# Causal self-attention: eleven score fills of the row maxima issued between the tiles of the projection

## The reference, cut to what matters

```python
def _attn(x, ln_w, ln_b, conv_w, attn_w, proj_w, n_head):
    h = _layernorm(x, ln_w, ln_b)
    ...
    qkv = h @ attn_w
    q, k, v = jnp.split(qkv, 3, axis=-1)
    ...
    q = q * cos + _rotate_half(q) * sin
    k = k * cos + _rotate_half(k) * sin
    scores = jnp.einsum('bqhd,bkhd->bhqk', q, k) / jnp.sqrt(jnp.float32(D))
    scores = jnp.where(causal, scores, jnp.float32(-1e+30))
    p = jax.nn.softmax(scores, axis=-1)
    y = jnp.einsum('bhqk,bkhd->bqhd', p, v).reshape(B, T, C)
    return y @ proj_w
```

## Time and profile before

| | |
|---|---|
| median of 3 runs | 2651.42 us (2646.68 to 2652.11) |
| the profiled execution | 2654.03 us |
| its span | 2652.2 us |
| mean granted clock of PE | 0.958 |
| PE, DVE, ACT, POOL busy | 85%, 74%, 69%, 50% of the span |
| projection, second half, batch 0 | 1682 to 1696.5 us |
| maxima, batch 0 | 1696.5 to 1786.6 us |
| projection, batch 1 | 1889 to 1926 us |
| maxima, batch 1 | 1926 to 2015.3 us |

### The profile page before, as it was taken

How to read it: one execution, slowest core, us unless ns; L and a number is a source line. 1 busy time by engine, 2 the same in 40 slices (tenths; PEclk the granted TensorE clock), 3 DMA queues, 4 the chain that set the end, 5 groups by cost and what they waited for, 6 DMA issues and landing times. The chain is left out here.

```text
span 2652.2 us, 38396 instructions
## 1 busy us (share of the span) xinstructions
PE 2257.2 (85%) x12302; PEld 1165.0 (44%) x12303; DVE 1974.4 (74%) x1868; ACT 1819.6 (69%) x2842; POOL 1328.6 (50%) x508
## 2 busy tenths in 40 slices
PE   7788888888888888888888897779978979999988
PEld 2344444444434444444444352323422255665547
DVE  6899999999978999999999458782384142225665
ACT  5899999999959999999999335207604731113256
POOL 2099998999942999989999212000000022110020
PEclk8899999999999999999999979879988979999999
DMA  2510001000015000010000012001000051001000
GB/s 91 139 44 28 28 28 40 28 28 27 24 74 135 29 26 25 28 41 27 28 28 21 18 48 84 1 1 38 28 1 25 25 231 69 24 22 38 0 10 32
DMA packets 57112, 110.27 MB, mean 42 GB/s; under 512 B 13123, under 2 KB 18499, under 8 KB 55984
## 3 DMA queue, kind: packets, MB, share of 16 engines
q1 hardware_dynamic: 48656, 97.58, 11.7%
q0 software_dynamic: 8352, 11.31, 1.5%
HBM read 84.97 MB, written 23.59 MB: 41 GB/s over the span
## 5 line engine op out<-in xcount | busy, mean ns | idle before, releaser
L1522 POOL TENSOR_TENSOR hs<-hs,c_bc 128x2048 f32<-128x2048 f32 x256 | 1166.7, 4557 | 60.5 <-DVE hs L1573 45.0
L1573 DVE TENSOR_TENSOR_SCAN hs<-decays,ps 128x512 f32<-128x512 f32 x512 | 610.9, 1216 | 28.8 <-ACT decays L1536 10.0
L1573 DVE TENSOR_TENSOR_SCAN hs<-decays,carry,ps 128x512 f32<-128x512 f32 x512 | 621.5, 1269 | 5.7 <-PE ps L1600 4.7
L1608 PE MATMUL ps<-hs,sel 128*64 128x512 f32 x2048 | 496.3, 605 | 16.7 <-POOL hs L1522 16.4
L1600 PE MATMUL ps<-ident,dbu_even 128*128 128x128 f32 x2048 | 296.3, 283 | 97.5 <-DVE hs L1573 64.1
L1600 PE MATMUL ps<-ident,dbu_odd 128*128 128x128 f32 x2048 | 294.8, 283 | 92.4 <-DVE hs L1573 61.5
L1536 ACT ACTIVATE decays<-delta_far,A 128x512 f32<-128x512 f32 x512 | 359.3, 715 | 7.3 <-DVE hs L1573 7.2
L1536 ACT ACTIVATE decays<-delta_near,A 128x512 f32<-128x512 f32 x512 | 360.2, 716 | 1.8 <-DVE hs L1573 1.8
L1544 ACT ACTIVATE dbu_odd<-du_turned,b_turned 128x512 f32<-128x512 f32 x512 | 359.5, 715 | 0.0
L1544 ACT ACTIVATE dbu_even<-du_turned,b_turned 128x512 f32<-128x512 f32 x496 | 348.4, 715 | 0.0
L1600 PEld LDWEIGHTS ps<-ident,dbu_even 128*128 128x128 f32 x2048 | 220.1, 142 | 248.1 <-DVE hs L1573 192.9
(11 more groups left out here) (338 smaller groups left out, 2623.4 us busy)
## 6 DMA issues: line engine op xcount, KB each, us to landing
c_bc<-c_rows SPq DMA_DIRECT2D x256, 128.0 KB, 2.9
o_rows<-osb SPq DMA_DIRECT2D x26, 256.0 KB
u_rows<-u SPq DMA_DIRECT2D x4, 1024.0 KB, 4.5
d_rows<-delta SPq DMA_DIRECT2D x4, 1024.0 KB, 4.2
delta_near<-d_rows SPq DMA_DIRECT2D x4, 1024.0 KB, 10.1
hs<-u_rows SPq DMA_DIRECT2D x4, 1024.0 KB, 6.7
delta_far<-d_rows SPq DMA_DIRECT2D x4, 1024.0 KB, 12.9
w_down<-in_expert_proj SPq DMA_DIRECT2D x1, 4096.0 KB, 31.8
```

The source lines that it names most:

```text
L1522: pool.tensor_tensor(x, x, spread(c_bc[:, g, :], 4), ALU.mult).then_inc(weighed.sem, 1)
L1573: dve.tensor_tensor_scan(hs[:, quad % RING, n, :], decays[:, s % RING, :], ps[:, DBU + s % RING, :], carry[:, at(i * GB, g), blk] if q els ...
L1608: mm = pe.matmul(ps[lo:lo + DB, ACC + quad % 2 * 2 + j // 2, :], k.sel2[:, :], hs[:, quad % RING, j, :], start=False, stop=False, skip_gro ...
```

## The change

The first eleven fills (those of query tiles 0 to 3) leave `maxima` and are issued inside `project`: fill f goes on PE right behind tile 13 + f, and its reduction on DVE right behind the take of that same tile. All eleven use banks 4 to 7, so the ring of the tiles is cut to banks 0 to 3. The first fill waits for the eight masked copies of the first half on ACT; each later fill waits for the reduction of the fill before it. `maxima` then starts with the fills of tile 4, and its transposition of the first maxima comes after two fills. The place of the normalisation of batch 0 (ahead of tile 8) stays. `negmax` is allocated earlier.

```diff
-def project(k, tiles, banks=8, pending=None, beside=()):
+def project(k, tiles, banks=8, pending=None, beside=(), ahead=None):
...
+    turn_of_pending = min(own, banks)
+    if ahead:
+        banks = ahead.bank
...
                 mm.then_inc(summed.sem, 1)
+                if ahead:
+                    ahead.by_tensor(pe, n)
...
-                elif pending and n == min(own, banks):
+                elif pending and n == turn_of_pending:
...
                         copy(eng).then_inc(followed.sem, 1)
+                if ahead and name == "dve":
+                    ahead.by_vector(eng, n)
...
+class EarlyFills:
+
+    def __init__(self, k, job, negmax, first, copies):
+        self.k, self.jobs, self.negmax, self.first, self.copies = k, [job], negmax, first, copies
+        self.fills = [fill for fill in plan_fills([job], T, True) if (fill[1] + 1) * P <= W]
+        self.scores_to = scores_by(self.fills)
+        self.bank = 8 - STRIPS
+        self.scored, self.maxed, self.followed = k.sig("scored"), k.sig("maxed"), k.sig("followed")
+
+    def by_tensor(self, pe, n):
+        f = n - self.first
+        if not 0 <= f < len(self.fills):
+            return
+        if f:
+            pe.wait_ge(self.maxed.sem, self.maxed.at(f))
+        else:
+            pe.wait_ge(self.followed.sem, self.followed.at(self.copies))
+        score_fill(self.k, pe, self.jobs, self.fills[f], self.bank, self.scored)
+
+    def by_vector(self, dve, n):
+        f = n - self.first
+        if not 0 <= f < len(self.fills):
+            return
+        dve.wait_ge(self.scored.sem, self.scored.at(self.scores_to[f]))
+        reduce_fill(self.k, dve, self.fills[f], self.bank, self.negmax).then_inc(self.maxed.sem, 1)
...
-def maxima(k, jobs, nk, causal, prob, negmax, later, ctx):
+def maxima(k, jobs, nk, causal, prob, negmax, first_fill, later, ctx):
...
+    fills = plan_fills(jobs, nk, causal)[first_fill:]
     PART = NJ * TILES // 2
-    early = 2 + max(f for f, (e, t, *_) in enumerate(fills) if e * TILES + t < PART)
+    early = 2 + max([f for f, (e, t, *_) in enumerate(fills) if e * TILES + t < PART], default=0)
...
-        project(k, tiles, pending=pending, beside=taps(HN, hcs, vec, 0) if b == 0 else ())
+        ahead = EarlyFills(k, job, negmax, len(tiles) // 2 + 1, 4 * C)
+        project(k, tiles, pending=pending, beside=taps(HN, hcs, vec, 0) if b == 0 else (), ahead=ahead)
```

More of the change, by code:

```diff
@@ L754, in _ @@
                 pending.fetch(sp)
+    if ahead:
+        ahead.passed()
     summed.passed(len(tiles))
@@ L1647, in __init__, with attention @@
         self.q, self.kk, self.v, self.out, self.masked = q, kk, v, out, False
-def attention(k, jobs, nk, causal, recip, root, lag, wo, ctx, beside=(), by_pe=0):
+def attention(k, jobs, nk, causal, recip, root, lag, wo, ctx, beside=(), by_pe=0, ahead=None):
     nc, ps = k.nc, k.ps
@@ L1666, in attention @@
     pick = k.sb("pick", [P, 2, 2, P], ctx=ctx) if by_pe else None
-    negmax = k.sb("negmax", [P, len(jobs), T // P, H], ctx=ctx)
+    negmax = ahead.negmax if ahead else k.sb("negmax", [P, len(jobs), T // P, H], ctx=ctx)
     later = MaxRows(k, jobs, negmax, rows, [k.sig(f"max_in{n}") for n in range(2)])
-    maxima(k, jobs, nk, causal, prob, negmax, later, ctx)
+    maxima(k, jobs, nk, causal, prob, negmax, len(ahead.fills) if ahead else 0, later, ctx)
     rows_turned, rows_copied = k.sig("rows_turned"), k.sig("rows_copied")
@@ L1943, in put_rows, with plan_fills @@
               .then_inc(self.max_in[part].sem, 16)
-def maxima(k, jobs, nk, causal, prob, negmax, later, ctx):
+STRIPS = 4
+def plan_fills(jobs, nk, causal):
+    fills = []
+    for e in range(len(jobs)):
+        for t in range(T // P):
+            n = (t + 1) * P if causal else nk
+            for o in range(0, n, W):
+                m = min(W, n - o)
+                per = 4 if m <= W // 4 else 2 if m <= W // 2 else 1
+                for g in range(0, 4, per):
+                    fills.append((e, t, o, m, W // per, range(g, g + per), causal and o + m == n))
+    return fills
@@ new lines, in scores_by, with score_fill @@
+def scores_by(fills):
+    return [STRIPS * sum(len(fill[5]) for fill in fills[:f + 1] if fill) for f in range(len(fills))]
+def score_fill(k, pe, jobs, fill, bank, scored):
+    ps = k.ps
+    e, t, o, m, room, groups, masked = fill
+    qx, kx = jobs[e].qx, jobs[e].kx
+    whole = masked and m == P
+    for j in range(STRIPS if whole else 0):
+        pe.matmul(ps[:, bank + j, :].rearrange("p (g n) -> p g n", g=W // P), k.ident16[:],
+                  spread(k.late_key[:], W // P), start=True, stop=False, skip_group_check=True)
+    for n, group in enumerate(groups):
+        c, par = divmod(group, 2)
+        at = n * room
+        for j in range(STRIPS):
+            strip = slice(32 * j, 32 * j + 32)
+            mm = pe.matmul(ps[:, bank + j, at:at + m], qx[strip, par, c, t * P:(t + 1) * P],
+                           kx[strip, par, c, o:o + m], start=not whole, stop=True, skip_group_check=whole)
+            if whole or not masked:
+                mm.then_inc(scored.sem, 1)
+        for j in range(STRIPS if masked and not whole else 0):
+            pe.matmul(ps[:, bank + j, at + m - P:at + m], k.ident16[:], k.late_key[:],
+                      start=False, stop=True, skip_group_check=True).then_inc(scored.sem, 1)
@@ new lines, in reduce_fill, with passed @@
+def reduce_fill(k, dve, fill, bank, negmax):
+    e, t, o, m, room, groups, _ = fill
+    per = len(groups)
+    banks = k.ps[:, bank:bank + STRIPS, 0:per * room].rearrange("p j (g n) -> p j g n", g=per)
+    to = negmax[:, e, t, :].rearrange("p (g j) -> p j g", j=STRIPS)
+    return dve.tensor_reduce(to[:, :, groups[0]:groups[0] + per], banks[:, :, :, 0:m], AX.X, ALU.max, negate=True)
+class EarlyFills:
[20 more added lines that the diff above has]
+        reduce_fill(self.k, dve, self.fills[f], self.bank, self.negmax).then_inc(self.maxed.sem, 1)
+    def passed(self):
+        self.scored.passed(self.scores_to[-1])
+        self.maxed.passed(len(self.fills))
@@ L1959, in maxima @@
     to_mask = [job for job in jobs if not job.masked]
[L1960 to L1968, removed]
+    fills = plan_fills(jobs, nk, causal)[first_fill:]
     PART = NJ * TILES // 2
-    early = 2 + max(f for f, (e, t, *_) in enumerate(fills) if e * TILES + t < PART)
+    early = 2 + max([f for f, (e, t, *_) in enumerate(fills) if e * TILES + t < PART], default=0)
     fills.insert(early, None)
     NF = len(fills)
-    scores_to = [STRIPS * sum(len(fill[5]) for fill in fills[:f + 1] if fill) for f in range(NF)]
+    scores_to = scores_by(fills)
     with ExitStack() as c2:
@@ L2008, in _ @@
                     continue
-                e, t, o, m, room, groups, masked = fill
-                qx, kx = jobs[e].qx, jobs[e].kx
+                e, t, o, _, _, groups, _ = fill
                 if to_mask and (t, o, groups[0]) == (0, 0, 0):
@@ L2015, in _ @@
                     pe.wait_ge(maxed.sem, maxed.at(f - 1))
[L2016 to L2031, removed]
+                score_fill(k, pe, jobs, fill, STRIPS * (f % 2), scored)
         @block.vector
@@ L2042, in _ @@
                     continue
[L2043 to L2047, removed]
                 dve.wait_ge(scored.sem, scored.at(scores_to[f]))
-                dve.tensor_reduce(to[:, :, groups[0]:groups[0] + per], banks[:, :, :, 0:m], AX.X, ALU.max,
-                                  negate=True).then_inc(maxed.sem, 1)
+                reduce_fill(k, dve, fill, STRIPS * (f % 2), far if fill[2] else negmax).then_inc(maxed.sem, 1)
             if WIDE:
```

4 lines of the change are left out of this document (2 added, 2 removed).

## The result

| | before | changed |
|---|---|---|
| median of 6 runs | 2652.14 us (2646.68 to 2654.34) | 2669.22 us (2664.09 to 2671.88) |
| profiled execution, its span | 2654.03, 2652.2 us | 2671.88, 2670.1 us |
| mean granted clock of PE | 0.958 | 0.959 |

The changed kernel takes 1.0063 times as long, 95% interval 1.0051 to 1.0075: 17.1 us slower by the medians. It was forecast 23 us slower, at 2674.4 us within 2663 to 2686.

What follows compares the result with a forecast made beforehand. DVE was taken to set the pace in the early fills, PE in the projection's second half. Losses of 6.7 (batch 0), 12.2 (batch 1) and 4 us (clock) made 22.9, say +23: 2674.4 us, range 2663 to 2686.

Steps and rivals of the forecast that it cites:

- The chain of round trips: Early fills: each fill waits for the reduction before it in one bank set; eleven take 41.2 us against 22.06 before.
- hand-overs: Between fills and reductions: about 0.06 us from DVE to PE and 0.03 us from PE to DVE, chosen values.
- What hides beside it: Early fills: a tile's matmuls under the reduction and its take under the fill cost nothing at the high clock.
- The early start: Batch 0, projection: fill 0 can start when ACT's last copy of the first half ends, at 1685.85.
- Batch 0: Its early fills and restart of the maxima: loss of 6.2 to 7.2 us, taken as 6.7.
- The restart: Start of the maxima block, batch 0: 0.33 us to PE, a 1.14 us fill, 0.03; tile 4's first reduction at 1728.5.
- Batch 1: Its early fills, four output tiles alone after them, and restart: loss of 11.7 to 12.7 us, taken as 12.2.
- The stop ahead of tile 12: Batch 1, projection: ring of four makes PE pause about 4.8 us until tile 8 is taken, hidden by ACT's copies.
- The clock: Early fills: low PE clock throughout would add some 11.4 us per batch; a fifth taken, 2 us per batch.
- the oscillating clock: Rival, early fills: pauses drop PE's clock again and again; half gives +30 us, 2682, all +42; chance 0.22.
- A give-back of the 9 us: Rival, remaining maxima: fills meet another clock phase and time comes back, +14 us, 2665; chance 0.10.
- The rival on the other side: Early fills: DVE still sets the pace, only busy time counts, -9 us, 2642, faster; chance 0.03.

Runs made afterwards that it cites:

- the experiment on the places: Changed kernel with batch 1's early fills set behind other tiles (13, 14, 15, 17, 19, 20, 21, 23 to 26): 2665.96 against 2650.04 us for the kernel before.
- The two experiments with one set: Kernel before, first eleven fills unmoved but sharing banks 0 to 3: 2701.58 us; the same with two extra matmuls behind each of the first ten: 2679.89 us.
- the two runs with half fills: Changed kernel, each early fill cut into two halves of two banks: 2673.38 us; the same with batch 1's fills also behind other tiles: 2678.29 us.

## Why the prediction was right, and where it was off

The sign and the mechanism were right, and the measured 2669.22 us lie in the range.

- **The chain of round trips** was put at 41.2 us for eleven. Less the first fill and the last reduction that is 36.6; measured 36.66, in both batches, and within 0.01 us in every run of this code. The hand-overs, chosen as 0.06 and 0.03 us, were right: the round shown above has 0.03 us from the end of the fill to the reduction, and 0.06 us from the end of the reduction (1718.49 + 2.29) to the next fill.
- **What hides beside it**: the tile's matmuls and its take, at no cost. Right; DVE waits for PE behind every take.
- **The early start** was forecast by starting fill 0 at 1685.85, 3.73 us after tile 12. It came 3.79 us after it (1679.62 and 1683.41 in the new trace).
- **Batch 0** was put at 6.7 us, between 6.2 and 7.2; the stage measured 8.5. The restart is the part that was short: the first fill of tile 4 was costed at the high clock and ran at the low one, so C was 4.8 us where 3.8 were summed, and the little that the new order was to save after it did not show in D.
- **Batch 1** was put at 12.2 and measured 12.6; C was forecast as 9.2 (1953.6 to 1962.8) and was 9.18. The 4.7 us of it that other places can hide were isolated by the experiment on the places. The stop ahead of tile 12 was there, 4.68 us where 4.8 were expected, and cost about 0.5 us where it was put at nothing: tiles 12 and 13 took 6.07 us, where 5.3 were put for a clock that fell; with the fills away the shorter ring costs 8 us.
- **The clock** was the term that failed: 4 us, taken as a fifth of 11.4 per batch for low phases inside the new stretch. That stretch ran at 0.98 and 1.00, and B did not vary, so the term is 0 there. The prediction saw in the pauses a danger. The two experiments with one set show both sides: with nothing between the fills the clock is 0.52 and B 48 us, with tiles or extra matmuls it is high and B 36.7. The tiles held the clock up. One term of the 11.4 is shown by no run as it stands: the 3.5 us of a query/key tile at the low clock, the author's estimate as twice the 1.76 at the high one. In the changed kernel tile 12 of batch 1 ran at 0.50 and DVE began to take it 3.82 us after its start; in the kernel before, at the high clock, it took the first of such tiles 1.92 us after its start (1682.12 to 1684.04).

The rest of the gap between +23 and +17 is not explained by a stage: the stages lose 21.1 us in the profiles, and the medians differ by 17.1, with an interval of 13.5 to 20 us from the ratio. Single profiles of the same code differ by 4 us, which is enough for it. So the near hit has some luck in it: the forecast had 4 us too much for the clock and 2.2 too little for the two batches.

Some figures beside the prediction's sum were wrong, and none of them enters it. It read from the earlier trace rows that DVE waited only twice for PE's scores. The same view has six more waits, on the reductions into `negmax_far`, five of them in this line:

```profile
DVE negmax_far L2049 <- PE ps L2030: 3.9, 5, 1.4
```

All but one of the eight lie behind the eleven fills, so the reading holds for the stretch that was changed and not for the whole maxima. And the new maxima block was put at some 62 us, where the prediction's own sum for batch 0 (from 1727.0 to 6.7 us behind 1786.6) gives 66; it took 67.7 and 66.1 us, from the end of DVE's last instruction of the projection to the end of the join. Hand-overs of 0.2 us each would have added 0.31 us to each of eleven rounds, so 3.4 us per batch and not 2. And the upper end of the forecast's own span, +28, has 8 us for the clock, for which no working is given.

Of the rivals, the oscillating clock did not come, though its condition, short pauses in every round, did. The rest of the maxima does swing between two levels: in the kernel before the clock was 1.00 from 1736 to 1740 and 0.50 from 1744 to 1748, and a mean of 0.77 between these two is the 46% of low time that the prediction names. The new stretch, with PE's pauses of 0.58 to 1.47 us ahead of the fills, stayed at 0.98 and 1.00. A give-back of the 9 us that were forecast did not come either: D was 64.97 and 64.26 us after 65.23 and 64.45; one of a few us can't be told from the spread of D. The rival on the other side would have needed B near 22 us. The second set of banks is worth 16.8 us of 36.7 per batch in this stage.

## What to carry to other kernels

Before work is moved under another stage, count what the buffers allow. The two engines that handed one set of banks back and forth here took the sum of their times, 36.7 us for B with tiles beside it or with extra matmuls, whatever idle time the stage around them offered; the 11 us won by an earlier start did not pay for the 17 lost by giving up the second set. And where a PE with pauses feeds a DVE that sets the pace, look at the granted clock: here, at 0.77 and 0.78, an extra matmul of 0.63 us in PE's pause of 1.06 brought 9.3 us, and one of 1.06 us, as long as the pause, brought nothing.

## What the runs showed of the hardware that was not expected

- Half the strips don't take half the time: fp32 score matmuls of 512 columns on two 32-row strips took 1.13 us, on four strips 1.14 us.
- Identical code of 27 fills (D) took 60.7 to 65.9 us from run to run, with granted clocks from 0.92 to 0.74 (60.7 us at 0.87, 65.9 at 0.74 in the two runs with half fills), while the chain B repeated to 0.02 us.
- Adding PE work made the kernel faster by 0.37% (0.24 to 0.51%): 256 extra columns ahead of 16 of the fills held the clock at 0.99, and 512 columns held it at 0.95 to 0.97 but gave the gain away again.
